# Four late clears of an adjacency table, issued as one block ahead of the third group's rows of B

## The reference, cut to what matters

```
h        = mish([x[src], x[dst], edge_attr] @ W1 + b1)
messages = mish(h @ W2 + b2)
agg      = segment_sum(messages, dst)
u        = mish([x, agg] @ W3 + b3);   y = x + u @ W4 + b4;   layernorm(y) * gamma + beta
```

## Time and profile before

| what | value |
|---|---|
| time, median of 3 | 1541.91 us |
| the profiled execution's own time | 1540.79 us |
| its span | 1539.1 us |
| TensorE busy | 1498.8 us (97%) |
| VectorE busy | 1414.7 us (92%) |
| ScalarE busy | 1296.5 us (84%) |
| GpSimd busy | 1082.4 us (70%) |
| DMA over the span | 133 GB/s |

### The profile page before, as it was taken

How to read it: one execution, slowest core, us unless ns; L and a number is a source line. 1 busy time by engine, 2 the same in 40 slices (tenths; PEclk the granted TensorE clock), 3 DMA queues, 4 the chain that set the end, 5 groups by cost and what they waited for, 6 DMA issues and landing times.

```text
span 1539.1 us, 33365 instructions
## 1 busy us (share of the span) xinstructions
PE 1498.8 (97%) x7862; PEld 1170.1 (76%) x7862; DVE 1414.7 (92%) x2922; ACT 1296.5 (84%) x2505; POOL 1082.4 (70%) x984
## 2 busy tenths in 40 slices
PE   7969999999999999999999999999999999999998
PEld 5747777777777777777777777777777777776785
DVE  7679999999999999999999999999999999995666
ACT  4058999999999999999999999999999999995462
POOL 1246888888888788787788887888878888762220
PEclk9979999999999999999999999999999999999999
DMA  8845555555554555544554555555555455455673
GB/s 310 306 138 142 125 118 122 124 119 117 124 123 116 123 123 115 127 117 115 126 119 116 127 121 117 121 124 118 118 122 124 116 123 124 112 136 127 137 146 151
DMA packets 122452, 205.10 MB, mean 133 GB/s; under 512 B 31641, under 2 KB 54297, under 8 KB 122416
## 3 DMA queue, kind: packets, MB, share of 16 engines
q0 software_dynamic: 59392, 116.85, 34.8%
q1 hardware_dynamic: 62672, 87.30, 18.2%
q10 hardware_dynamic: 352, 0.52, 0.1%
HBM read 151.60 MB, written 42.75 MB: 126 GB/s over the span
## 4 chain that ended last, share of the span: by engine, by line
PE 81%; issue 5%; DVE 4%; POOL 4%; DMA 3%; ACT 1%; POOLq 1%; DVEq 0%; SPq 0%; ACTq 0%
PE bm L1070 48%; PE bp L1049 6%; PE bp L1057 5%; PE bs L1093 4%; PE bp L1059 4%; PE pu L336 2%; PE pm L1081 2%; PE pu L1998 2%; PE po L2020 2%; PE pB L679 2%; DMA xg<-A_tab,idx 1%; PE pm L1080 1%; POOL hTl L974 1%; POOL M_tab L999 1%; POOL agg_tab L988 1%
## 5 line engine op out<-in xcount | busy, mean ns | idle before, releaser
L974 POOL TENSOR_TENSOR hTl<-tp,hTh 128x512 fp32r<-128x512 f32 (+1 forms) x314 | 411.0, 1309 | 224.5 <-DVE khl L1261 203.5
L1070 PE MATMUL bm<-W2h,hTh 128*128 128x512 f32 x1252 | 498.4, 398 | 2.2 <-POOL hTl L974 1.7
L1070 PE MATMUL bm<-W2l,hTh 128*128 128x512 f32 x1252 | 497.0, 397 | 0.0
L1070 PE MATMUL bm<-W2h,hTl 128*128 128x512 f32 x1252 | 494.5, 395 | 0.0
L963 POOL DMA_INDIRECT xg<-A_tab,idx x305 | 319.4, 1047 | 49.5 <-issue 39.1
L1070 PEld LDWEIGHTS bm<-W2h,hTh 128*128 128x128 f32 x1252 | 235.5, 188 | 71.7 <-DVE bm L1254 14.8
L1131 ACT ACTIVATE rp<-bp 128x512 f32<-128x512 f32 (+1 forms) x314 | 183.3, 584 | 116.8 <-PE bp L1059 115.7
L1070 PEld LDWEIGHTS bm<-W2l,hTh 128*128 128x128 f32 x1252 | 235.6, 188 | 57.5
L1070 PEld LDWEIGHTS bm<-W2h,hTl 128*128 128x128 f32 x1252 | 235.6, 188 | 53.7
L1225 DVE SCALAR_TENSOR_TENSOR rp<-rp 128x512 f32<-128x512 f32 (+1 forms) x314 | 215.6, 687 | 38.7 <-ACT rp L1131 25.8
L1235 DVE SCALAR_TENSOR_TENSOR tp<-rp,bp 128x512 f32<-128x512 f32 (+1 forms) x314 | 211.7, 674 | 4.5 <-ACT rp L1137 2.2
(11 more groups left out here) (244 smaller groups left out, 2318.9 us busy)
## 6 DMA issues: line engine op xcount, KB each, us to landing
ea<-in_eaT SPq DMA_DIRECT2D x156, 128.0 KB
M_tab<-mev POOLq DMA_DIRECT2D x157, 80.0 KB
agg_tab<-ev POOLq DMA_DIRECT2D x157, 64.0 KB
db<-in_dst_rows SPq DMA_DIRECT2D x78, 128.0 KB
M<-M SPq DMA_DIRECT2D x76, 128.0 KB
xg<-A_tab,idx POOLq DMA_INDIRECT x313
eaW<-Bh_tab SPq DMA_DIRECT2D x77, 64.0 KB
eaW<-Bl_tab SPq DMA_DIRECT2D x77, 64.0 KB
```

The source lines that it names most:

```text
L974: e.tensor_tensor(hTl[p][:, j, 0:w], pick(u, start_t, tp)[:, 0:w], hTh[p][:, j, 0:w], ALU.subtract)\
L1070: last = e.matmul(bank[0:r, :], a[p][:, c, j * P:j * P + r], w[:, c, :], start=False, stop=c == KC - 1 and w is W2l, skip_group_check=True)
```

## The change

SyncE's `loads` is cut in two: `inputs` (indices, edge attributes, destinations) and `window` (rows of B and the copy of M2). For the third group the order is now `inputs`, all four late clears, `window`; the four waits for counts of `products` are gone. The fourth group's loads follow undivided, with no clear behind them. Every later group is as before, and no other engine's program is touched.

```diff
-            def loads(u):
+            def inputs(u):
...
                 e.dma_start(db[p][:, 0:n], dst_rows[bass.ds(u.group(), 1), 0:n].to_broadcast([64, n]))\
                  .then_inc(q_in[p], 16)
+
+            def window(u):
+
+                p, n = u.par, ETAIL if tail(u) else G
                 b = e.value_load(base_i[0:1, bass.ds(u.group(3), 1)], min_val=0, max_val=NP - WIN)
                 wait(e, s_pre, u.val(1, -4))
                 rows(e, p, b)
                 e.wait_ge(s_prep, u.group(2, 1))
                 copy(e, p, n)
 
+            def loads(u):
+
+                inputs(u)
+                window(u)
+
             e.wait_ge(s_pre, 1)
-            loads(At(None, 8))
-            for i, n in zip(range(M_EARLY, NCH), (6, 7, 9, 10)):
-                if n == 9:
-                    loads(At(None, 12))
-                e.wait_ge(s_pre, n)
+            inputs(At(None, 8))
+            for i in range(M_EARLY, NCH):
                 zero_m(e, i, q_zlate)
+            window(At(None, 8))
+            loads(At(None, 12))
```

## The result

The changed kernel takes 1536.77 us, the median of 7 runs (1534.78 to 1540.57), against 1541.91 (1540.08 to 1542.75, 7 runs). The ratio of the new time to the old is 0.9971, 95% interval 0.9960 to 0.9982: 4.5 us less, 2.8 to 6.2 by the interval (the two medians alone differ by 5.1). Forecast: 1537.3, 4.6 less. Beside two later batches the same kernel gave ratios of 0.9967 (0.9954 to 0.9979) and 0.9976 (0.9966 to 0.9985).

A forecast was written before the change was run, and what follows sets the result against it. TensorE, busy 97% of the span, was taken as the bound, its stop before chunk 8 costing 7.50 us. Earlier landing 2.8 plus clock 1.85 gave 4.65 us off 1541.9: 1537.3 us, with 8 in 10 for 1535.0 to 1541.2.

The forecast's parts named there:

- What holds the gather: Before chunk 8: two clears of 640 KB fill the DMA about 3.5 us, so the last gather takes 5.93 us.
- Rival 1: The clears are not what holds the gather; at most about 0.5 us comes back, 1541.4 us; chance 0.17.
- The landing: Third group's fourth gather lands at 107.8, TensorE starts chunk 8 at 107.9 instead of 110.67: gain 2.8 us.
- clean row: A later gather without clears beside it, issued at 122.58, data ended by 125.5: 2.9 us after the issue.
- The clears in the gap: Four clears, 2.62 MB, flow in the nearly empty DMA stretch, about 89.6 to 96.7, at 373 GB/s.
- The clock: After the stop before chunk 8: clock stays up, 2.71 us back, or falls, 1.0 back; half each, value 1.85.
- The second pair, the window, the waits: Moving the later two clears, rows of B behind the clears, and dropping waits for finished products: each worth 0.
- What is late next: VectorE's bias copy after chunk 8 starts ends at 112.2, needed at 112.6: margin 0.4 us.
- The sum: 2.8 us from the earlier start plus 1.85 from the clock: 4.65 us less, forecast 1537.3 us.

The follow-up runs named there:

- the dose: All four clears in the old place of the first two, behind the third group's copy of M2, no waits between, against the kernel before: 1543.00 us, ratio 1.0014.
- before_gathers_early: Kernel before the change, clears in their old places, all four gathers of the third group issued in step -1: 1538.65 us, ratio 0.9980.
- second_pair: Only the second pair of clears moved into the gap, the first kept in its old place, against the kernel before: 1541.34 us, ratio 1.0001.
- rows_first: Changed kernel with the third group's rows of B ahead of the four clears: 1537.87 us, ratio 0.9975 to the kernel before.
- gathers_alone: As gathers_early, but SyncE holds the fourth group's loads until the third group's gathers have landed: 1536.48 us, ratio 0.9968 to the kernel before.
- after: The changed kernel without further edit, against the kernel before: 1536.77 us, ratio 0.9971.
- first_pair: Only the first pair of clears moved into the gap, the second kept behind the fourth group's loads, against the kernel before: 1537.54 us, ratio 0.9981.
- gathers_early: Changed kernel with all four gathers of the third group issued in step -1: 1536.31 us, ratio 0.9962 to the kernel before.
- before: The kernel without the change, to which the ratios refer: median 1541.91 us.

## Why the prediction was right

- **What holds the gather.** Right: the two pairs alone and the dose show that the first pair's place does it. For the late gather the prediction named only the clears' own bytes; the fourth group's loads, pushed by them onto the last gather, have a part in it that it did not count. Rival 1, with at most 0.5 us to come back, is out. The Trainium skill's rule ("DMA: Bandwidth & Descriptors", "Queues, rings and completion order") of going round the queues packet by packet did not bring an equal share, neither of bytes nor of the trace's packets: GpSimd's queue had 0.12 of 1.31 MB in 46 of 961 packets, and 0.37 of 2.35 MB with four clears. Whether the trace's packets are those of the rule no run here shows.
- **The landing.** Predicted 107.8 and a start at 107.9; 107.97 and 108.11 came. The gather's 3.2 us were 3.40. Gain 2.56 in place of 2.8, of which 0.04 is an earlier issue. The near hit is partly luck. The clean row's 2.9 us ran to the gather's last data, not to its landing, and the 0.3 were put on for other traffic. In the profile after the last data came 3.0 us behind the issue, as in that row, and the landing 0.4 us behind them: that tail is the term that was missing.
- **The clears in the gap.** Predicted to flow from 89.6 to 96.7 at 373 GB/s; 89.6 to 97 ran at 359. SyncE got the four off in 4.24 us, between the two values given, and the rows of B went out at 93.48 and 94.39, five us later than before, with nobody waiting.
- **The clock.** I gave each outcome half, 2.71 or 1.0 us back. Of six profiles with a stop of 2.2 to 2.7 us, two kept the clock (step 3.86) and four lost it (5.31 to 5.42, so 1.45 to 1.56 more; I had 1.7). My reason for the half was wrong. I bounded it by an idle time of 1.35 us that left the clock up and one of 2.14 us behind which it was down. Behind the same 1.35 us the clock fell in the profile after, and behind a stop of 3.49 us it stayed up (before_gathers_early). So an idle time's length alone doesn't decide, in either direction; that the half came near was luck. The Trainium skill ("TensorE: Matmul & The Clock Gate", section "Part 1: The HAM clock gate") says that the number of slow matmuls at a kernel's start varies from run to run for the same kernel. These profiles show such a variation behind a stop in the middle of a kernel.
- **The second pair, the window, the waits.** All set at 0. Moving the second pair alone gave 1.0001 (second_pair), and the window's place showed no cost (rows_first). The waits were not tested alone.
- **What is late next.** The bias copy was forecast to end at 112.2 and needed at 112.6; in the profile after it ran 111.76 to 112.45, needed at 112.84. The margin of 0.4 us was right, and gathers_alone shows it used up.

```profile
111.76 0.69 DVE L1262 COPY bm<-b2b 128x512 f32<-128x512 f32 x1
```

- **The sum.** 4.6 forecast; 4.5 by the ratio. The two profiles by themselves would have given 5.25 for this place and 4.02 in all, and the difference is the clock's fall 1360 us later. The profile after is one in which the clock stayed up at the stop, so it shows nearly the whole 2.71 back; with two of six that kept it, the mean over the six is 1.6 to 1.7 us, and the 1.85 was near that.

## What to carry to other kernels

A bulk transfer that nobody waits for can still set the time, if it flows while another queue's small transfer is what the bound engine (the one whose work sets the time) wants next: look for the stretch in which that transfer took longer than its like elsewhere, and see which queue had the bytes. Move such a block into a stretch where the DMA engines are idle and no short-deadline transfer follows within its length; its order against other loads of its own queue matters only if their cover is shorter than the block. And a change that shortens a stop of TensorE's should be judged over several profiles, since each short stop may or may not cost a slow stretch as well. When the landing of a transfer is estimated from rows of its data, add the tail from its last data to the waiting engine's start, here 0.5 us and more.

## What the runs showed that I had not expected

- The same idle time of 1.35 us in the last stages was followed by 24 matmuls in 5.8 us in nine of the twelve profiles and in 7.36 in three (after, first_pair, gathers_early), where the clock fell. With it and the stop before chunk 8, executions of one kernel can differ by 1.5 or 3 us. The runs of after spread over 5.8 us (1534.78 to 1540.57), those of before beside them over 2.7, and 31 later runs of before over 5.8 as well; what makes the rest of the spread is open.
- Of four gathers issued in a row beside 0.48 MB of other loads the last is put at 5.70 us to its landing, nearly as beside the clears (5.93): counted from TensorE's first product, the issue came 3.3 us sooner (101.63 - 84.70 against 104.57 - 84.33) and TensorE's start 1.0 us (107.47 - 84.70 against 108.11 - 84.33).
